# Reordering one pipelined iteration of a gated recurrence and feed-forward kernel: half of the W_out product at the iteration's end, new orders on every engine

## The reference, cut to what matters

```python
u = x @ W_in + b_in
g = sigmoid(x @ W_gate + b_gate)
h_t = tanh(h_prev @ A + u_t @ Bm)            # over t
y_t = h_t @ C.T + u_t @ D.T
y_t = g_t * y_t + (1.0 - g_t) * x_t
x1 = layernorm(x + (ys @ W_out + b_out + x))
hidden = gelu(x1 @ bw1.T + b1)               # bw: signs of w times a row's mean |w|
out = layernorm(x1 + (hidden @ bw2.T + b2))
```

## Time and profile before

| | before |
|---|---|
| median of three runs | 446.37 us |
| profiled execution, its own time | 446.38 us |
| its span | 444.6 us |
| TensorE busy | 424.6 us (96%) |
| VectorE busy | 361.0 us (81%) |
| ScalarE busy | 309.9 us (70%) |
| GpSimd busy | 302.3 us (68%) |

### The profile page before, as it was taken

The page is one execution under the profiler, slowest core; times in us unless marked ns, Lnnn a source line. Parts: engine busy times, 40 slices in busy tenths (PEclk is TensorE's granted clock), DMA queues, the critical chain, the costliest instruction groups (busy, mean ns, idle before and its releaser), DMA issues.

```text
span 444.6 us, 8039 instructions
## 1 busy us (share of the span) xinstructions
PE 424.6 (96%) x2687; PEld 303.4 (68%) x2687; DVE 361.0 (81%) x791; ACT 309.9 (70%) x570; POOL 302.3 (68%) x302
## 2 busy tenths in 40 slices
PE   7999999999998899999999999999999999999882
PEld 4788887777554576776867767677676776766651
DVE  3666687744772889999999999999999999998584
ACT  1222224656446768798898988989889898797791
POOL 5199722242467697977979779797797977683523
PEclk9999999999999999999999999999999999999998
DMA  7944550000110112133331342313423134231222
GB/s 225 361 137 132 142 136 2 1 0 1 47 48 2 47 34 63 47 50 112 74 100 48 97 118 73 96 48 97 122 68 97 55 88 129 63 97 46 51 94 94
DMA packets 43893, 37.16 MB, mean 84 GB/s; under 512 B 35504, under 2 KB 37296, under 8 KB 43856
## 3 DMA queue, kind: packets, MB, share of 16 engines
q1 hardware_dynamic: 42528, 35.66, 28.7%
q0 software_dynamic: 272, 0.66, 0.6%
q10 hardware_dynamic: 1056, 0.36, 0.3%
HBM read 19.90 MB, written 8.39 MB: 64 GB/s over the span
## 4 chain that ended last, share of the span: by engine, by line
PE 59%; DVE 19%; POOL 8%; issue 5%; ACT 4%; DMA 4%; SPq 0%; DVEq 0%; POOLq 0%; ACTq 0%
PE bank L1016 15%; PE bank L1004 12%; PE bank L978 8%; PE bank L862 7%; DVE hid L1328 7%; PE bank L774 6%; PE bank L767 5%; DMA gT<-in_L_attn_x 4%; DVE bank L1311 3%; ACT hid L631 3%; DVE gT L1341 3%; PE bank L759 3%; PE bank L960 2%; DVE bank L1334 2%; DVE gT L1323 2%
## 5 line engine op out<-in xcount | busy, mean ns | idle before, releaser
L1004 PE MATMUL bank<-xT,w1s 128*128 128x512 f16 x512 | 127.1, 380 | 4.5 <-DVE hid L1328 3.8
L1016 PE MATMUL bank<-w2s,hid 128*128 128x256 f16 x1024 | 125.4, 273 | 1.1 <-DVE gT L1341 1.0
L1016 PEld LDWEIGHTS bank<-w2s,hid 128*128 128x128 f16 x1024 | 98.6, 98 | 31.6 <-issue 5.9
L623 ACT ACTIVATE bank<-bank,b_col,alpha 128x512 f32<-128x512 f32 x128 | 96.8, 756 | 18.8 <-PE bank L1004 18.4
L1328 DVE SCALAR_TENSOR_TENSOR hid<-bank,small,hid 128x512 f16<-128x512 f32 x128 | 94.4, 739 | 14.3 <-ACT hid L631 14.3
L631 ACT ACTIVATE hid<-bank,small 128x512 f16<-128x512 f32 x128 | 86.6, 692 | 19.0 <-PE bank L1016 17.8
L1004 PEld LDWEIGHTS bank<-xT,w1s 128*128 128x128 f16 x512 | 45.9, 98 | 51.1 <-DVE hid L1328 9.9
L407 POOL TENSOR_TENSOR ys_lo<-gT,ys_hi 128x512 fp32r<-128x512 f32 x32 | 40.8, 1277 | 26.3 <-ACT ys_hi L598 26.2
L403 POOL TENSOR_TENSOR gT<-gT,xT 128x512 f32<-128x512 f32 x32 | 40.8, 1276 | 24.4 <-DVE gT L1283 24.3
L774 PE MATMUL bank<-hu,w_rec 128*128 128x128 f32 x208 | 45.5, 300 | 1.0 <-DVE hu L1125 0.9
L423 POOL TENSOR_TENSOR gT<-x_rows,b_row 128x1024 f32<-128x1024 f32 x16 | 38.1, 2379 | 7.7 <-DMA xT<-gT 7.7
(11 more groups left out here) (135 smaller groups left out, 802.0 us busy)
## 6 DMA issues: line engine op xcount, KB each, us to landing
x_load<-in_L_attn_x SPq DMA_DIRECT2D x16, 512.0 KB, 3.5
gT<-in_L_attn_x SPq DMA_DIRECT2D x15, 512.0 KB, 3.7
out_rows<-gT SPq DMA_DIRECT2D x15, 512.0 KB, 2.6
gT<-in_L_ffn_w SPq DMA_DIRECT2D x2, 1024.0 KB, 12.1
gT<-in_L_attn_x SPq DMA_DIRECT2D x4, 128.0 KB, 2.9
out_rows<-gT SPq DMA_DIRECT2D x2, 256.0 KB, 2.0
xT<-gT SPq DMA_TRANSPOSE x28, 3.2
w_gate<-in_L_attn_W_gate ACTq DMA_DIRECT2D x1, 256.0 KB, 7.8
```

The source lines that it names most:

```text
L623: nc.scalar.activation(bank[which][:, :], bank[which][:, :], ACT.Gelu, bias=b1_col[:, c:c + 1], scale=alpha1[:, c:c + 1]).then_inc(s_gelu, 1)
L1004: done = nc.tensor.matmul(bank[which][:, :], w1s[:, c, k, :], x1T[:, n, :, part, :, k, :], start=(k == 0 and part == 0), stop=(k == KD - 1 ...
L1016: done = nc.tensor.matmul(bank[tile // 2][:, tile % 2 * DM:(tile % 2 + 1) * DM], hid[:, c % 3, part, tile * P:(tile + 1) * P], w2s[:, :, c ...
```

## The change

No instruction is added or removed. On SP the transposes of group n+1 are issued ahead of the store of group n-3. On TensorE F4 and H7 come before `out_products(n + 2, 0)`, which so ends the iteration and stands next to `y_products` and `out_products(., 1)` of the next; H6 is moved ahead of F3. On GpSimd `second_rstd` moves to the front, `first_rstd` and `residual` behind the second `mix`. ScalarE and VectorE have new orders throughout.

```diff
@@ SP
-                if due(n - 3) and n - 3 < NB - 3:
-                    store(n - 3)
                 if due(n + 1) and n + 1 >= TURNED:
                     for pair in range(2):
                         turn(n + 1, pair)
+                if due(n - 3) and n - 3 < NB - 3:
+                    store(n - 3)
@@ GpSimd
                     mix(n + 2, 0)
-                if due(n):
-                    residual(n)
-                if due(n + 1):
-                    first_rstd(n + 1, 0)
+                if due(n - 2):
+                    second_rstd(n - 2, ALL_TILES, n - 1, n * 2 - 4)
                 if due(n + 3):
-                    pool.wait_ge(s_rs1, n * 2 + 3)
+                    pool.wait_ge(s_rs2, n - 1)
                     hu_low(n + 3, 0)
                     hu_low(n + 3, 1)
                 if due(n + 2):
                     mix(n + 2, 1)
                 if due(n + 1):
+                    first_rstd(n + 1, 0)
                     first_rstd(n + 1, 1)
+                if due(n):
+                    residual(n)
                 if due(n + 2):
                     ys_low(n + 2, 0)
-                if due(n - 2):
-                    second_rstd(n - 2, ALL_TILES, n - 1, n * 2 - 4)
-                if due(n + 2):
                     ys_low(n + 2, 1)
@@ ScalarE
+                if due(n - 1):
+                    hidden_gelu(n - 1, 6)
+                    hidden_gelu(n - 1, 7)
+                    hidden_hi(n - 1, 6)
                 if due(n - 3):
                     second_norm(n - 3, 1)
-                if due(n - 1):
-                    hidden_gelu(n - 1, 6)
-                    hidden_hi(n - 1, 6)
-                    hidden_gelu(n - 1, 7)
-                if due(n - 3):
-                    second_norm(n - 3, 2)
                 if due(n - 1):
                     hidden_hi(n - 1, 7)
                 if due(n + 3):
                     hu_high(n + 3, 0)
-                    hu_high(n + 3, 1)
+                if due(n - 3):
+                    second_norm(n - 3, 2)
                 if due(n):
                     hidden_gelu(n, 0)
-                    hidden_hi(n, 0)
-                if due(n + 1):
-                    x1_hi(n + 1, 0)
                 if due(n + 2):
                     ys_high(n + 2, 0)
                 if due(n):
-                    hidden_gelu(n, 1)
-                    hidden_hi(n, 1)
-                    hidden_gelu(n, 2)
+                    hidden_hi(n, 0)
+                if due(n + 3):
+                    hu_high(n + 3, 1)
                 if due(n - 3):
                     second_norm(n - 3, 3)
+                if due(n - 2):
+                    second_norm(n - 2, 0)
                 if due(n):
+                    hidden_gelu(n, 1)
+                    hidden_gelu(n, 2)
+                    hidden_hi(n, 1)
+                    hidden_gelu(n, 3)
                     hidden_hi(n, 2)
-                    hidden_gelu(n, 3)
+                if due(n + 2):
+                    ys_high(n + 2, 1)
+                if due(n):
+                    hidden_hi(n, 3)
+                    hidden_gelu(n, 4)
+                if due(n + 1):
+                    x1_hi(n + 1, 0)
...
@@ TensorE
                     ffn_out(n, 2)
+                    hidden(n, 6)
                     ffn_out(n, 3)
-                    hidden(n, 6)
+                    ffn_out(n, 4)
+                    hidden(n, 7)
                 if due(n + 2):
                     out_products(n + 2, 0)
-                if due(n):
-                    hidden(n, 7)
-                    ffn_out(n, 4)
@@ VectorE, from hidden_lo(n, 0) on
                     second_sum(n - 1, 0)
                     second_sum(n - 1, 1)
+                if due(n + 1):
+                    first_moments(n + 1, 1)
                 if due(n):
                     hidden_lo(n, 1)
+                    hidden_lo(n, 2)
                 if due(n + 1):
+                    first_norm(n + 1, 0)
                     first_norm(n + 1, 1)
+                if due(n):
+                    hidden_lo(n, 3)
+                if due(n + 1):
                     x1_lo(n + 1, 0)
                 if due(n):
-                    hidden_lo(n, 2)
+                    hidden_lo(n, 4)
                 if due(n + 1):
                     x1_lo(n + 1, 1)
-                if due(n):
-                    hidden_lo(n, 3)
+                if due(n + 3):
+                    less_x(n + 3, 0)
                 if due(n - 1):
                     second_spread(n - 1, 0)
...
```

More of the change, by code:

```diff
@@ L663, in iteration @@
                 if due(n):
-                    hidden_gelu(n, 1)
-                    hidden_hi(n, 1)
-                    hidden_gelu(n, 2)
+                    hidden_hi(n, 0)
+                if due(n + 3):
+                    hu_high(n + 3, 1)
                 if due(n - 3):
                     second_norm(n - 3, 3)
+                if due(n - 2):
+                    second_norm(n - 2, 0)
                 if due(n):
+                    hidden_gelu(n, 1)
+                    hidden_gelu(n, 2)
+                    hidden_hi(n, 1)
+                    hidden_gelu(n, 3)
                     hidden_hi(n, 2)
-                    hidden_gelu(n, 3)
+                if due(n + 2):
[6 more added lines that the diff above has]
+                if due(n):
+                    hidden_hi(n, 4)
                 if due(n + 1):
@@ L674, in iteration @@
                 if due(n):
-                    hidden_hi(n, 3)
-                if due(n + 2):
-                    ys_high(n + 2, 1)
-                if due(n):
-                    hidden_gelu(n, 4)
+                    hidden_gelu(n, 5)
                 if due(n + 1):
@@ L682, in iteration @@
                 if due(n):
-                    hidden_gelu(n, 5)
-                    hidden_hi(n, 4)
                     hidden_hi(n, 5)
@@ L687, in iteration @@
                     x1_copy(n + 1, 1)
-                if due(n - 2):
-                    second_norm(n - 2, 0)
             gate(GATED, 1)
@@ L1363, in iteration @@
                     first_sum(n + 1, 0)
-                    first_spread(n + 1, 0)
                 if due(n - 1):
                     hidden_lo(n - 1, 6)
-                if due(n + 1):
-                    first_moments(n + 1, 0)
                 if due(n + 2):
@@ L1373, in iteration @@
                 if due(n + 1):
+                    first_spread(n + 1, 0)
                     first_sum(n + 1, 1)
-                    first_norm(n + 1, 0)
-                    first_spread(n + 1, 1)
                 if due(n + 2):
@@ L1379, in iteration @@
                 if due(n + 1):
-                    first_moments(n + 1, 1)
+                    first_spread(n + 1, 1)
+                    first_moments(n + 1, 0)
                 if due(n):
@@ L1401, in iteration @@
                 if due(n + 3):
-                    less_x(n + 3, 0)
+                    gate_y(n + 3, 0)
                 if due(n - 1):
                     second_spread(n - 1, 1)
[L1405 to L1408, removed]
                 if due(n):
```

## The result

| | before | changed |
|---|---|---|
| median (8 runs each) | 446.34 us | 451.01 us |
| profiled execution, own time | 446.38 us | 450.93 us |
| its span | 444.6 us | 449.1 us |
| F5 to F5 in the middle of the run | 18.41 us | 18.86 us |

The changed kernel takes 1.0115 times as long, 95% interval 1.0092 to 1.0139: slower, as forecast, by 4.7 us instead of 3.3.

The account below looks back on a forecast made before the run. The prediction took TensorE to bound the kernel, with 18.21 of 18.41 us an iteration its own work. Terms of +3.9, -1.0, -0.1 and +0.5 gave +3.3 us on 446.38: 449.7 us, range 446.2 to 451.7.

Parts of the forecast that it names:

- The chain and its clock: From F6's end (zero), ScalarE's hi(0) to hi(2) delays lo(1) and lo(3), making H4 and H6 late.
- The size of an iteration: Iterations 3 to 12: H6 0.59 us late, 18.80 instead of 18.41 us each, +3.9 us over ten.
- The half tile: `hu_high(., 1)` on ScalarE loses its overlap with both neighbours: 0.69 us behind hi(0), 0.66 to the next operation.
- the rival without it: The half tile overlaps as usual on ScalarE: 18.57 us an iteration, 447.3 us in all, no change; chance 0.22.
- Iterations 1 and 2: Start of the run: -1.0 us in iteration 1, -0.1 us in iteration 2.
- Iterations 13 and 14: End of the run: waits level within 0.05 us in 13, H(15, 0) late by +0.5 us in 14.
- The 0.5 of iteration 14: `x1_lo` ends near 10.3 behind F6's end, so H(15, 0) can't start before 13.6 instead of 13.1: +0.5 us.
- My step: At the end of the run, 3.3 us for the transposes from the last `x1_lo` to H, from the earlier trace.
- None of these adds to it: Behind the late H6, F4, the transposes (14.1, wanted at 16) and VectorE's next lo(0) (0.2 to spare) cost nothing.
- Three H with the first y start the same way: TensorE's timeline: three H up to the first y take 2.62 us from start to start, like three F.
- The vanished wait on the other side: ScalarE's stretch is short enough, H5's 0.20 us wait goes: 18.21 us an iteration, 443.3 us; chance 0.11.
- The further wait: VectorE's 0.2 us margin at lo(0) or `hu_low`'s 0.4 is missed, 0.2 on ten iterations: 451.7 us; chance 0.12.

Follow-up runs that it names:

- e1_half_back: Changed kernel with `hu_high(n+3, 1)` on ScalarE moved back beside `hu_high(n+3, 0)`, out of the stretch from hi(0) to hi(2): 445.52 us, 0.9989 of before.
- e5_norm_moved: Changed kernel with `second_norm(n-2, 0)` on ScalarE back at the iteration's end, the half tile left in the stretch: 445.98 us, 1.0005 of before.
- e7_repaired: Changed kernel with `hu_high(n+3, 1)` back beside half 0, SP's old order, and one `second_norm` and g3 moved behind hi(2) on ScalarE: 442.83 us, 0.9943 of before.
- e2_store_first: Changed kernel with SP's old order, the store ahead of the two transposes: 450.03 us, 1.0099 of before.
- e4_halves_swapped_b: Changed kernel with the halves of `hu_high` and `hu_low` swapped from group 4 on, lower half in ScalarE's stretch: 447.44 us, 1.0037 of before.
- e9_one_turn_at_a_time: Changed kernel with SP issuing a group's second transpose only when the first has landed: 472.95 us, one run.
- e6: Kernel before with SP's new order alone, the store behind the transposes: 445.74 us, 1.0000 of before.
- e3: Kernel before with TensorE's new order alone: 460.25 us, one run.
- e8: Repaired kernel (e7_repaired) with `x1_hi(n+1, 1)` ahead of hi(4) and `x1_lo(n+1, 1)` ahead of lo(4) in iterations 13 and 14: 442.50 us, 0.9928 of before.

## Why the prediction was right, point by point

**The chain and its clock: right.** The end of F6 starts it, ScalarE from hi(0) to hi(2) sets it, and it ends in H4 and H6. e1_half_back and e5_norm_moved shorten it by two different operations and give 18.40 both times. Both keep TensorE's new order, and e7_repaired keeps it at 18.18, which rules out that this order by itself makes the wait; e2_store_first, still at 18.87, rules out SP's.

**The size of an iteration: 0.45 instead of 0.39.** H4 at 5.30 behind zero instead of 5.25, H6 at 9.02 instead of 8.96. hi(2) starts at 5.02 instead of 5.00, and the steps from there to H6 add 0.04 more; no single spacing is off by more than 0.02, the half tile's with 0.71 instead of 0.69. Ten iterations make 0.6 us of it.

**The half tile: right, and narrower than I put it.** One instance from before the iterations carried the term, and with it the difference between slower and unchanged (the rival without it gave 447.3 us); that it held was not certain. e4_halves_swapped_b shows that it isn't the half tile as such but the upper half.

**Iterations 1 and 2: right** within 0.1 us (-0.90 and -0.02 for -1.0 and -0.1).

**Iterations 13 and 14: the term that was too small.** "In 13 ... the waits come out level" is right up to H6, which is 0.87 us late there, as H5 was 0.89 before. It left out H(14, 0), whose wait of 0.51 for its transposes is the whole of the 0.50. The 0.5 of iteration 14 was 0.84. My step took 3.3 us from the last `x1_lo` to H. In iteration 13 it was 5.1: the transposes' landing of the earlier trace rows was taken for a constant, and it isn't. In iteration 14 it was 3.6: the landing was 3.2 and the second issue started 0.43 us late, 1.7 us behind the first. In all five kernels with SP's new order the last two issues take 2.90 us together, in the five with the old order (e9_one_turn_at_a_time apart) 2.61 or 2.62. So the store's place has to do with it, though nothing here shows how.

**The total.** The forecast of +3.3 us met +4.5 of span and +4.7 between the medians. The terms behind F5 of iteration 1 came to +4.9; that the first part of the profiled run was 0.4 us quicker is luck, and makes the forecast look better than its terms.

**"None of these adds to it": right for the middle of the run.** With 4.7 us of landing the transposes still end 0.5 us ahead of H(n+1, 0) there. The 2 us to spare that I gave were mostly used up.

**Two readings to correct, which change no term.** "Three H with the first y start the same way" isn't so: y starts 2.41 behind the first H and not 2.62. F0 stands 3.29 behind that H, so y's three matmuls take the 0.67 that three H at 2.62 leave, y is shown about 0.2 early, and `hu_low` had more cover than 0.4. And of ScalarE's idle time in an iteration only 1.05 us waits for F6; 0.75 stands ahead of g0 and waits for H0.

**The rivals.** The vanished wait on the other side did not come, for the reason stated: its price was ScalarE's order. It is what e7_repaired makes of it, 442.83 us for the 443.3 that the rival named. The further wait came as the transfers at the end and not at GpSimd's `hu_low`, which cost TensorE nothing.

**Still open:** why the transposes land in 4.7 us with the new orders. It isn't SP's order (e2, e6), nor, for the first of a pair, two in flight (e9), nor TensorE's order alone, where the page shows 3.2 as well. What most of the traces have in common is the place: issued 6.2 to 6.6 us behind zero (before, e3, e6) they land in 3.2 in 13 of 14 iterations; issued 8.9 to 9.6 behind it (changed, e1, e2, e4, e5, e7, e8, and the first of each pair in e9) mostly in 4 to 5; and the second of e9, issued at 14.3, in 3.1. That is an agreement and no cause shown, and it has exceptions. Within e1_half_back two iterations of the same order land in 3.2 and others in 4.8, with the engines' timelines the same to 0.01 us, and in the last iteration they land in 3.1 to 3.3 in every kernel. Nothing was run to move the place alone.

## What to carry to other kernels

An engine that is idle for a tenth of a loop can still set its length. Find the event that restarts the chain, here the end of one matmul group, and count only what stands between it and the instruction that another engine needs next; everything else can be moved behind that. When the bottleneck's order is changed, a new consumer (here H6, moved ahead of one F) has an earlier due time, and each engine's stretch up to it has to be added up again.

## What the runs showed of the hardware

ScalarE overlaps neighbouring activations by about 0.1 us when they begin at the same partition, be they 64 or 128 partitions high (0.59 and 0.52 from start to start, with durations of 0.69 and 0.62), and by nothing when one that begins at partition 64 stands between two that begin at 0 (0.71 and 0.65, with 0.69 and 0.63). The issue of one of these DMA transposes holds SP for 1.23 us or more, and in no pair did the second start less than about 1.3 us behind the first. They land in 3.1 to 3.4 us or in some 4 to 5.5, and one execution can have both.
